# Normalising z2 on ScalarE instead of VectorE, and adding one with a two-tensor operation, in a gated cross-attention and mixture-of-experts kernel

## The chip, the cores and the metric

One Trainium2 chip (trn2), one core. The metric is device time in microseconds, lower is better. A run is one launch of the whole kernel; the time of a kernel is the median of its runs.

## The reference

For each of B = 32 sequences of S = 112 rows and D = 256 columns the kernel computes a gated cross-attention on a context of 375 rows, adds it to x, and then runs a mixture of eight experts (each row takes its best two) on the normalised result:

```
x = x + tanh(g_xattn[0]) * xattn(ctx, layernorm(x), mask)    # 8 heads of 64, keys = context and latents
z2 = layernorm(x)                                            # (x - mean) / sqrt(var + eps)
bids = sigmoid(z2 @ conf_w.T + conf_b) * wealth              # 8 experts
top_bids, chosen = top_k(bids, 2);  weights = softmax(top_bids)
x = x + tanh(g_ffn[0]) * sum over chosen experts of weight * (silu(z2 Wg) * (z2 Wu)) Wd
```

## The kernel before

Everything on the five engines is written out by hand with semaphores; the order of each engine's instructions is the order of the text. There are two stages.

The **attention stage** (to about 1150 us of the span) is a loop over sequences, called batches here, two to an iteration of the loop (parity `p`). A turn of `body(b, p)` has eight steps `h`, one per head. In step h the engines work on several batches at once: TensorE (PE) makes the scores of batch b (`sims`, tile simP), the projections of batch b + 1 (`piece`, tile fP), the transposes of the probabilities (`probs_T`, ptP) and the products with the values (`values`, oP) of heads two and three back, and it finishes batch b - 1: transposing the heads' outputs (`heads_T`), the output projection (`out_proj`), and in step 7 the transpose of z2 (`norm2_T`, line 1271). VectorE (DVE) takes the masked maximum of the scores (`masked_max`, L833), on which the exponentials on ScalarE (ACT, L635) wait, and it makes the low halves of every split number (L823, L839). PE's `sims` of the next batch wait for the masked maximum of head 7 of this one (semaphore s_max).

The **path to z2** of batch b - 1: in step 5 VectorE adds the residual, takes the statistics (L863 to L870: x1, then mean and variance in mv1); GpSimd (POOL) makes 1/sqrt(var + eps) in rs1 (`rstd1`, L464 and L467); in step 6 VectorE normalises x1 to z2 (`norm2`, L876); in step 7 PE transposes z2 (L1271). Behind `rstd1` in POOL's own order stands `split_weights`: two long instructions (L474, L477) that split a 128x1536 piece of the experts' weights into a high and a low part, one piece per batch. ScalarE in step 6 normalises the second half of a later batch's rows (`norm_rows`, L602 and L603).

The **routing** is done for a pair of batches, in odd turns from b = 3 on: VectorE's chain `choose` (steps 2 to 4), `route_rank` (step 5), `route_weights` (step 6, L936 to L943: small tiles of 112x2 and 112x16) and `route_place` (step 7), each link waiting for the one before. `route_weights` stands ahead of the masked maximum of head 7 in VectorE's order.

The **expert stage** then runs 63 tiles of 128 routed rows through the experts, weights streamed by DMA.

The tiles of the change: `rs1` (per row: var + eps, 1/sqrt), `mv1`, `x1`, `z2` (printed as z in the profile), `gexp` and `w1` (printed as w), and `ones`, a tile of ones in SBUF that the kernel already has.

Of the kernel before, what the change touches and what calls it, by code (L numbers as in the profile page):

```python
# [5 lines left out]
F32 = mybir.dt.float32  # L6
# [4 lines left out]
ALU = mybir.AluOpType  # L11
ACT = mybir.ActivationFunctionType
# [3 lines left out]
B, S, D = 32, 112, 256  # L16
# [48 lines left out]
def build(nc, x, ctxt, mask, scal, lnw, wqkv, wout, confw, confbw, wffn, out):  # L65
# [4 lines left out]
    with ctx:  # L70
        def sem(name):
            return ctx.enter_context(nc.semaphore(name))

        def sb(name, shape, dt, stack=ctx):
            return stack.enter_context(nc.sbuf_tensor(name, shape, dt))

        def psum(name, shape, stack):
# [6 lines left out]
        minus_half = sb("minus_half", [P, 4], F32)  # L84
# [33 lines left out]
        x1 = [sb(f"x1_{i}", [S, D], F32) for i in range(2)]  # L118
# [13 lines left out]
        gexp = sb("gexp", [S, 2], F32)  # L132
        w1 = sb("w1", [S, 2], F32)
# [6 lines left out]
        pa = ExitStack()  # L140
# [16 lines left out]
        ones = sb("ones", [P, P], F32, pa)  # L157
# [25 lines left out]
        aoT = sb("aoT", [P, 2, MB, S], F32R, pa)  # L183
        bn1 = sb("bn1", [S, 6], F32, pa)
        mv1 = sb("mv1", [S, 2], F32, pa)
        rs1 = sb("rs1", [S, 2], F32, pa)
        z2 = [sb(f"z2_{i}", [S, D], F32, pa) for i in range(2)]
        z2T = sb("z2T", [P, KD, S], F32, pa)
        wstage = wr[:, :, :].rearrange("p a c -> p (a c)")[:, 0:WCH]
# [54 lines left out]
        s_bn1, s_mv1, s_rch1, s_rs1, s_z2, s_z2t, s_z2c, s_logit, s_lg = [sem(n) for n in (  # L244
            "s_bn1", "s_mv1", "s_rch1", "s_rs1", "s_z2", "s_z2t", "s_z2c", "s_logit", "s_lg")]

        s_rexp, s_route, s_oh, s_gexp, s_rank, s_slots, s_zcopy, s_scat = [sem(n) for n in (
            "s_rexp", "s_route", "s_oh", "s_gexp", "s_rank", "s_slots", "s_zcopy", "s_scat")]
# [11 lines left out]
        def need(eng, semaphore, count):  # L260

            if not isinstance(count, int) or count > 0:
                eng.wait_ge(semaphore, count)

        def apart(eng):

            eng.sem_inc(s_carry, 1)

        def holds(b, lo, hi):

            return lo <= b <= hi if isinstance(b, int) else True
# [7 lines left out]
        def zseq(b, k):  # L279

            return k if isinstance(b, int) and b == 0 else seq(b - 2, PZ + k)
# [112 lines left out]
        def _(pool):  # L394
# [66 lines left out]
            def rstd1(b):  # L461
                pool.wait_ge(s_mv1, b + 1)
                apart(pool)
                nc.gpsimd.tensor_scalar(rs1[:, 0:1], mv1[:, 1:2], EPS, None, ALU.add).then_inc(s_rch1, 1)  # L464
                pool.wait_ge(s_rch1, b + 1)
                apart(pool)
                nc.gpsimd.tensor_tensor(rs1[:, 1:2], rs1[:, 0:1], minus_half[0:S, 0:1], ALU.pow).then_inc(s_rs1, 1)  # L467

            def split_weights(b):

# [105 lines left out]
        def _(act):  # L576
# [17 lines left out]
            def norm_rows(b, p, part):  # L594

                if part == 0:
                    act.wait_ge(s_rstd, b + 1)
                    need(act, s_piece, 0 if isinstance(b, int) and b == 0 else zseq(b - 1, KD - 1) + 1)
                    for i in range(2):
                        nc.scalar.activation(z[0:CP, i, :], xc[p][:, i, :], ACT.Identity, bias=shift[0:CP, i:i + 1], scale=rs[0:CP, i:i + 1])  # L600
                else:
                    nc.scalar.activation(z[0:CP, 2, :], xc[p][:, 2, :], ACT.Identity, bias=shift[0:CP, 2:3], scale=rs[0:CP, 2:3])  # L602
                    nc.scalar.activation(z[0:S, 3, :], xl[p][:, :], ACT.Identity, bias=shift[0:S, 3:4], scale=rs[0:S, 3:4]).then_inc(s_z, 1)  # L603
# [40 lines left out]
            def heads_out_hi(b):  # L644
                act.wait_ge(s_aot, b + 1)
                nc.scalar.activation(aoT[:, 0, :, :], aoT_P, ACT.Copy).then_inc(s_aohi, 1)

            def norm2_out(b):
                act.wait_ge(s_z2t, b + 1)
                nc.scalar.activation(z2T[:, :, :], z2T_P, ACT.Copy).then_inc(s_z2c, 1)  # L650
# [18 lines left out]
            def body(b, p, last_pair=None):  # L669
                for h in range(H):  # L670
                    if h == 4 and holds(b, 1, B):
                        heads_out_hi(b - 1)
                    if holds(b, 0, B - 3):
                        if h == 1:
                            rows_out(b + 2)
                        if h == 2:
                            rows_hi(b + 2, p)
                    if holds(b, 0, B - 2):
                        for n in SLOT_PIECES.get(h, []):
                            piece_hi(b + 1, 1 - p, n)  # L680
                    if h < 2 and holds(b, 1, B):
                        probs_hi(b - 1, H - 2 + h)
                    if h >= 2 and holds(b, 0, B - 1):
                        probs_hi(b, h - 2)
                    if holds(b, 0, B - 1):
                        exps(b, p, h)
                    if h == 7 and holds(b, 1, B):
                        norm2_out(b - 1)
                    if h in (5, 6) and holds(b, 0, B - 4):
                        norm_rows(b + 3, 1 - p, h - 5)  # L690
                    if h == 5 and holds(b, 2, B + 1):
                        copy_rows(b - 2, p, (b - 2) // 2 if isinstance(b, int) else last_pair)
                    if p == 1 and holds(b, 3, B + 1):
                        pair_ = (b - 3) // 2 if isinstance(b, int) else last_pair
                        if h == 1:
                            route_exps(pair_)
                        if h == 5:
                            route_gap(pair_)
# [71 lines left out]
        def _(dve):  # L770
# [98 lines left out]
                apart(dve)  # L869
                nc.vector.bn_aggr(mv1[:, :], bn1[:, :]).then_inc(s_mv1, 1)  # L870

            def norm2(b, p):

                dve.wait_ge(s_rs1, b + 1)
                need(dve, s_zcopy, b - 1)
                nc.vector.tensor_scalar(z2[p][:, :], x1[p][:, :], mv1[:, 0:1], rs1[:, 1:2], ALU.subtract, ALU.mult).then_inc(s_z2, 1)  # L876

            def per_expert(ap):
                return ap.unsqueeze(1).to_broadcast([S, 2, E])

# [9 lines left out]
            def link(ins):  # L890
                chain[0] += 1
                ins.then_inc(s_route, 1)
# [40 lines left out]
            def route_weights(pair):  # L933

                dve.wait_ge(s_gexp, pair + 1)
                link(nc.vector.tensor_scalar(w1[:, :], gexp[:, :], 1.0, None, ALU.add))  # L936
                after_last(pair)
                link(nc.vector.tensor_tensor(slot[:, :, :], tmp[:, :, :], per_expert(regoff_b[:, :]), ALU.add))
                link(nc.vector.reciprocal(w1[:, :], w1[:, :]))
                after_last(pair)  # L940
                link(nc.vector.tensor_scalar(wt[:, 0, :], w1[:, :], gates[0:S, 1:2], None, ALU.mult))
                after_last(pair)
                link(nc.vector.tensor_tensor(wt[:, 1, :], wt[:, 0, :], gexp[:, :], ALU.mult))  # L943
# [50 lines left out]
            def body(b, p, j=None):  # L994
                for h in range(H):
# [23 lines left out]
                            piece_lo(b + 1, 1 - p, n)  # L1019
                    if h == 4 and holds(b, 1, B):  # L1020
                        heads_out_lo(b - 1)
                    if h == 6 and holds(b, 1, B):
                        norm2(b - 1, 1 - p)
                    choose_some(1)
                    if h == 5 and routing:

# [436 lines left out]
```

## Time and profile before

| | us |
|---|---|
| median of 3 runs | 1826.02 (1825.33 to 1826.6) |
| the profiled execution: time | 1822.79 |
| its span, first to last instruction | 1821.2 |
| TensorE busy | 1618.4 (89%) |
| VectorE busy | 1015.1 (56%) |
| ScalarE busy | 844.4 (46%) |
| GpSimd busy | 611.8 (34%) |
| mean granted clock of TensorE, as a share of its full speed | 0.92 |

The span is what the rows of the trace cover; the 1.6 us between it and the time of the same execution lie around it. An engine's busy time says how much it worked, not who waited for it: for that the waits and the order of time are read. Reading the clock: 1.00 means 2.4 GHz, 0.50 means 1.2 GHz, a number between them is a stretch with some of both.

### The profile page before, as it was taken

To read this page: it belongs to the slowest core of one execution; us is meant where nothing else is said; L and a number is where in the kernel's file an instruction comes from. 1 tells how busy PE (TensorE), PEld (TensorE's weight loads), DVE (VectorE), ACT (ScalarE), POOL (GpSimd) and SP (SyncE) were. 2 spreads that over 40 slices of the span, in tenths; PEclk is the share of its full clock that TensorE was granted. 3 is DMA by queue.
4 is the path that set the end of the run, shared out by engine and by line. 5 is a ranking of instruction groups with operands and counts; after the bars stand their busy time and mean duration, and the time that the engine had idled before them with its cause. 6 is when DMAs were issued, how large, how long until landed. Compare 5 with 4: busy or idle time off the path is not lost.

```text
span 1821.2 us, 39638 instructions
## 1 busy us (share of the span) xinstructions
PE 1618.4 (89%) x11946; PEld 1378.0 (76%) x11947; DVE 1015.1 (56%) x2655; ACT 844.4 (46%) x1856; POOL 611.8 (34%) x663
## 2 busy tenths in 40 slices
PE   1898988988988988988988987699999989999965
PEld 1687877877877877877877876578888878888855
DVE  4478678678678678678678666322333223333321
ACT  2576656656656656656656644222333222332221
POOL 4344434434434434434434432112222222222211
PEclk9899889889889889889889887799999999999987
DMA  2142322422322322322322324681111375111173
GB/s 88 44 137 73 137 88 75 134 86 78 131 86 79 130 86 79 131 85 80 130 85 81 114 103 138 215 254 26 29 26 29 89 236 167 26 26 29 28 213 95
DMA packets 70908, 180.59 MB, mean 99 GB/s; under 512 B 11664, under 2 KB 33552, under 8 KB 70864
## 3 DMA queue, kind: packets, MB, share of 16 engines
q1 hardware_dynamic: 54464, 153.66, 25.3%
q0 software_dynamic: 15264, 24.25, 6.6%
q10 hardware_dynamic: 1136, 2.12, 0.4%
q8 instruction: 24, 0.39, 0.1%
q14 instruction: 20, 0.16, 0.0%
HBM read 106.91 MB, written 73.09 MB: 99 GB/s over the span
## 4 chain that ended last, share of the span: by engine, by line
PE 68%; DVE 11%; DMA 7%; issue 7%; ACT 4%; POOL 1%; SPq 1%; DVEq 0%; POOLq 0%; ACTq 0%
PE fP L1184 19%; PE yP L1184 9%; PE gP L1184 8%; PE uP L1184 8%; PE simP L1232 5%; PE ptP L1242 4%; DMA W<-split_experts 3%; PE oP L1184 3%; PE aP L1370 2%; PE tP L1184 2%; DVE w L936 2%; DVE z L876 2%; DMA out<-ysb,xt 2%; PE fP L1200 2%; DMA xt<-routed_rows 1%
## 5 line engine op out<-in xcount | busy, mean ns | idle before, releaser
L1184 PE MATMUL fP<-zTs,ws 128*128 128x112 f32 (+1 forms) x1536 | 324.5, 369 | 1.0 <-DVE zT L810 0.9
L1184 PEld LDWEIGHTS fP<-zTs,ws 128*128 128x128 f32 x1536 | 261.7, 222 | 51.8 <-issue 31.1
L1123 DVE TENSOR_TENSOR act_h<-uP,sg 128x512 f32<-128x512 f32 x126 | 87.1, 691 | 289.2 <-ACT sg L731 289.2
L1184 PE MATMUL gP<-W,xT 128*128 (+1 forms) x756 | 210.9, 415 | 33.5 <-issue 27.0
L1184 PE MATMUL fP<-ws,zTs 128*122 128x512 f32 x768 | 207.2, 405 | 4.7 <-DVE kT L823 4.7
L731 ACT ACTIVATE sg<-gP 128x512 f32<-128x512 f32 x126 | 75.3, 597 | 289.9 <-PE uP L1184 289.9
L635 ACT ACTIVATE pr<-ms,nmax 112x488 f32<-112x488 f32 x256 | 179.3, 700 | 65.4 <-DVE nmax L833 65.2
L1184 PEld LDWEIGHTS yP<-W,aT 128*128 128x128 f32 x1512 | 192.5, 194 | 10.1 <-issue 5.3
L1184 PE MATMUL yP<-W,aT 128*128 (+1 forms) x1512 | 194.3, 286 | 4.6 <-DVE aT L1127 4.6
L1184 PE MATMUL uP<-W,xT 128*128 (+1 forms) x756 | 196.1, 395 | 0.0
L547 POOL DMA_INDIRECT out<-ysb,xt x63 | 100.6, 1596 | 270.5 <-ACT ysb L743 254.7
L833 DVE CUSTOM_DVE_ANT_0 ms<-simP,madd 112x488 f32<-112x488 f32 x256 | 169.4, 662 | 30.3 <-PE simP L1232 14.7
L1232 PE MATMUL simP<-kT,qT 64*112 64x488 f32 x768 | 135.5, 463 | 55.0 <-DVE nmax L833 54.4
L1184 PEld LDWEIGHTS gP<-W,xT 128*128 128x128 f32 x756 | 135.7, 192 | 59.8 <-issue 37.6
L1127 DVE TENSOR_TENSOR aT<-aP,aT 128x512 fp32r<-128x512 f32 x126 | 86.4, 686 | 164.7 <-ACT aT L737 164.7
L839 DVE SCALAR_TENSOR_TENSOR pT<-ptP,pT 122x448 f16<-122x448 f32 x256 | 157.9, 617 | 31.1 <-ACT pT L642 22.6
L642 ACT ACTIVATE pT<-ptP 122x448 f16<-122x448 f32 x256 | 138.2, 540 | 73.7 <-PE ptP L1242 65.2
L1184 PEld LDWEIGHTS uP<-W,xT 128*128 128x128 f32 x756 | 145.1, 192 | 32.2
L1184 PEld LDWEIGHTS fP<-ws,zTs 128*122 128x122 f32 x768 | 133.1, 183 | 45.8 <-issue 12.4
L1184 PE MATMUL oP<-v,pT 122*128 122x64 f16 x3072 | 142.8, 199 | 15.5 <-DVE ao L851 13.8
L737 ACT ACTIVATE aT<-aP 128x512 fp32r<-128x512 f32 x126 | 75.0, 595 | 172.4 <-PE aP L1370 172.4
L1242 PE MATMUL ptP<-ident,pr 112*122 112x112 f32 x1024 | 154.6, 277 | 0.0
(196 smaller groups left out, 2508.3 us busy)
## 6 DMA issues: line engine op xcount, KB each, us to landing
split_experts<-wparts SPq DMA_DIRECT2D x32, 1536.0 KB
W<-split_experts SPq DMA_DIRECT2D x64, 768.0 KB
wr<-wffn SPq DMA_DIRECT2D x32, 768.0 KB
xc<-ctxt SPq DMA_DIRECT2D x32, 375.0 KB
xt<-routed_rows POOLq DMA_DIRECT2D x63, 129.0 KB, 2.4
xl<-x SPq DMA_DIRECT2D x32, 112.0 KB
xres<-x SPq DMA_DIRECT2D x32, 112.0 KB, 7.9
out<-x SPq DMA_DIRECT2D x32, 112.0 KB, 1.9
```

The lines of the kernel that those rows point to most:

```text
L547: pool.indirect_dma_start(out[:, :], bass.IndirectOffsetOnAxis(ap=xt[k][:, D:D + 1].bitcast(I32), axis=0), ysb[k % 2][:, :], None, compute ...
L635: nc.scalar.activation(pr[h % 2][:, :], ms[h % 2][:, :], ACT.Exp, bias=nmax[p][:, h:h + 1], scale=-1.0, accum_out=rsum[p][:, h:h + 1]).the ...
L642: nc.scalar.activation(pT[h % 2][:, 0, :, 0:S], ptP[h % 2][0:KR, :, 0:S], ACT.Copy, scale=P_TOP).then_inc(s_pthi, 1)
L731: nc.scalar.activation(sg[i][:, :], gP[i][:, :], ACT.Silu).then_inc(s_silu, 1)
L737: nc.scalar.activation(aT[q][i][:, 0, :, :], aP[i][:, :, :], ACT.Copy).then_inc(s_athi, 1)
L833: nc.vector.tensor_tensor_reduce(out=ms[h % 2][:, :], in0=simP[h % 2][0:S, 0:NK], in1=madd[p][:, :], scale=-SCALE, scalar=3.0e38, op0=ALU. ...
L839: nc.vector.scalar_tensor_tensor(out=pT[h % 2][:, 1, :, 0:S], in0=ptP[h % 2][0:KR, :, 0:S], scalar=P_TOP, in1=pT[h % 2][:, 0, :, 0:S], op0 ...
L1123: nc.vector.tensor_tensor(act_h[i][:, :], uP[i][:, :], sg[i][:, :], ALU.mult).then_inc(s_act, 1)
L1127: nc.vector.tensor_tensor(aT[q][i][:, 1, :, :], aP[i][:, :, :], aT[q][i][:, 0, :, :].bitcast(F32), ALU.subtract).then_inc(s_atlo, 1)
L1184: last = nc.tensor.matmul(o, lhs(k, a), rhs(k, c), start=n == 0, stop=n == len(todo) - 1)
L1232: last = nc.tensor.matmul(simP[i][0:S, 0:NK], qT[p][r, a, h // 2, :], kT[p][r, c, h // 2, :], start=t == 0, stop=t == len(PARTS) - 1)
L1242: last = nc.tensor.transpose(ptP[h % 2][0:KR, c, 0:S], pr[h % 2][:, c * KR:(c + 1) * KR], ident[0:S, 0:S])
```

## The change

Four things are changed.

- `norm2` moves from VectorE to ScalarE. It was (x1 - mean) * rstd as one `tensor_scalar`; it becomes an activation with a scale and a bias per row, x1 * rstd + (-mean * rstd).
- GpSimd's `rstd1` gets two more small instructions that make the bias (mean * rstd, then times -1) in a third column of rs1, each waiting for the one before.
- On ScalarE `norm2` stands at the end of step 6, behind the exponentials and `norm_rows`; on VectorE it stood in step 6 behind `piece_lo` and ahead of `probs_lo`.
- In `route_weights` the addition of 1.0 to gexp, a `tensor_scalar`, becomes a `tensor_tensor` of gexp and a 112x2 part of `ones`.

```
-        rs1 = sb("rs1", [S, 2], F32, pa)
+        rs1 = sb("rs1", [S, 3], F32, pa)
...
                 nc.gpsimd.tensor_scalar(rs1[:, 0:1], mv1[:, 1:2], EPS, None, ALU.add).then_inc(s_rch1, 1)
-                pool.wait_ge(s_rch1, b + 1)
+                pool.wait_ge(s_rch1, b * 3 + 1)
                 apart(pool)
-                nc.gpsimd.tensor_tensor(rs1[:, 1:2], rs1[:, 0:1], minus_half[0:S, 0:1], ALU.pow).then_inc(s_rs1, 1)
+                nc.gpsimd.tensor_tensor(rs1[:, 1:2], rs1[:, 0:1], minus_half[0:S, 0:1], ALU.pow).then_inc(s_rch1, 1)
+                pool.wait_ge(s_rch1, b * 3 + 2)
+                nc.gpsimd.tensor_tensor(rs1[:, 2:3], mv1[:, 0:1], rs1[:, 1:2], ALU.mult).then_inc(s_rch1, 1)
+                pool.wait_ge(s_rch1, b * 3 + 3)
+                apart(pool)
+                nc.gpsimd.tensor_scalar(rs1[:, 2:3], rs1[:, 2:3], -1.0, None, ALU.mult).then_inc(s_rs1, 1)
...
+            def norm2(b, p):
+
+                act.wait_ge(s_rs1, b + 1)
+                nc.scalar.activation(z2[p][:, :], x1[p][:, :], ACT.Identity, bias=rs1[:, 2:3], scale=rs1[:, 1:2]).then_inc(s_z2, 1)
...
                     if h in (5, 6) and holds(b, 0, B - 4):
                         norm_rows(b + 3, 1 - p, h - 5)
+                    if h == 6 and holds(b, 1, B):
+                        norm2(b - 1, 1 - p)
...
-            def norm2(b, p):
-
-                dve.wait_ge(s_rs1, b + 1)
-                need(dve, s_zcopy, b - 1)
-                nc.vector.tensor_scalar(z2[p][:, :], x1[p][:, :], mv1[:, 0:1], rs1[:, 1:2], ALU.subtract, ALU.mult).then_inc(s_z2, 1)
-
...
-                link(nc.vector.tensor_scalar(w1[:, :], gexp[:, :], 1.0, None, ALU.add))
+                link(nc.vector.tensor_tensor(w1[:, :], gexp[:, :], ones[0:S, 0:2], ALU.add))
...
                     if h == 4 and holds(b, 1, B):
                         heads_out_lo(b - 1)
-                    if h == 6 and holds(b, 1, B):
-                        norm2(b - 1, 1 - p)
                     choose_some(1)
```

VectorE in the loop, steps 6 and 7 of an odd turn, before the change:

```order
L823 TENSOR_TENSOR v<-fP,v 122x512 [waits s_phi]
L876 TENSOR_SCALAR z_0<-x_0,mv,rs 112x256 [waits s_zcopy,s_rs1]
L839 SCALAR_TENSOR_TENSOR pT<-ptP,pT 122x4x112 [waits s_pthi]
L936 TENSOR_SCALAR w<-gexp 112x2 [waits s_gexp]
L263 REGISTER_ALU
L938 TENSOR_TENSOR slot<-tmp,regoff_b 112x16 [waits s_route]
L939 RECIPROCAL w<-w 112x2
```

L876 is the instruction that leaves this engine, and L936 the one that is rewritten. The same place with the change, up to the masked maximum of head 7:

```order
L835 TENSOR_TENSOR v<-fP,v 122x512 [waits s_phi]
L851 SCALAR_TENSOR_TENSOR pT<-ptP,pT 122x4x112 [waits s_pthi]
L942 TENSOR_TENSOR w<-gexp,ones 112x2 [waits s_gexp]
L263 REGISTER_ALU
L944 TENSOR_TENSOR slot<-tmp,regoff_b 112x16 [waits s_route]
L945 RECIPROCAL w<-w 112x2
L263 REGISTER_ALU
L947 TENSOR_SCALAR wt<-w,gates 112x2 [waits s_route]
L263 REGISTER_ALU
L949 TENSOR_TENSOR wt<-wt,gexp 112x2 [waits s_route]
L840 REGISTER_ALU
L845 ISA ms,nmax<-simP,madd 112x488 [waits s_sim,s_exp]
```

The normalisation of z2 (z_0<-x_0) is gone, and the first link of `route_weights` has two inputs; the four links behind it are as they were.

ScalarE in the loop, steps 6 and 7 of an odd turn, with the change (exponentials of head 6, then the second half of `norm_rows`, then step 7):

```order
L640 ACTIVATE pr,rsum<-ms,nmax 112x488 [waits s_pt,s_max]
L607 ACTIVATE z<-xc,shift,rs 125x256
L608 ACTIVATE z<-xl,shift,rs 112x256
L656 ACTIVATE z_0<-x_0,rs 112x256 [waits s_rs1]
L625 REGISTER_ALU
L633 ACTIVATE v<-fP 122x512 [waits s_piece]
L647 ACTIVATE pT<-ptP 122x4x112 [waits s_pv,s_pt]
```

L656 is the added instruction; the others stand as before.

GpSimd in the loop, `rstd1` and `split_weights` of an odd turn, with the change:

```order
L464 TENSOR_SCALAR rs<-mv 112x1 [waits s_mv1]
L465 ISA
L467 TENSOR_TENSOR rs<-rs,minus_half 112x1 [waits s_rch1]
L468 REGISTER_ALU
L469 TENSOR_TENSOR rs<-mv,rs 112x1 [waits s_rch1]
L470 REGISTER_ALU
L472 TENSOR_SCALAR rs<-rs 112x1 [waits s_rch1]
L476 ISA
L479 CAST wparts<-wr 128x1536 [waits s_wst,s_wput]
L482 TENSOR_TENSOR wparts<-wr,wparts 128x1536 [waits s_whi]
```

L469 and L472 are new, and stand ahead of the two long instructions of `split_weights` (L474 and L477 before).

## Rows read from the trace of the kernel before

**Rows 1.** The page, part 1: busy time, share, instructions of each engine.
```profile
PE 1618.4 (89%) x11946; PEld 1378.0 (76%) x11947; DVE 1015.1 (56%) x2655; ACT 844.4 (46%) x1856; POOL 611.8 (34%) x663
```

**Rows 2.** The waits: who waited for whom; us in total, times, longest.
```profile
PE simP L1232 <- DVE nmax L833: 54.4, 14, 4.0
PE tP L1271 <- DVE z L876: 19.3, 31, 5.0
```

**Rows 3.** Timeline, an odd turn: start us, duration us, instruction [idle before <-releaser].
```profile
516.27 1.47 POOL L474 CAST wparts<-wr 128x1536 fp32r<-128x1536 f32 x1
516.48 1.40 DVE L876 TENSOR_SCALAR z<-x,mv,rs 112x256 f32<-112x256 f32 x1
...
517.34 0.59 ACT L603 ACTIVATE z<-xl,shift,rs 112x256 f32<-112x256 f32 x1
...
517.91 3.43 POOL L477 TENSOR_TENSOR wparts<-wr,wparts 128x1536 fp32r<-128x1536 f32 x1 [0.18 <-POOL wparts L474]
...
517.94 0.41 PE L1271 MATMUL tP<-ident,z 112*128 112x112 f32 x2 [0.54 <-DVE z L876]
...
518.34 3.03 DVE L936 TENSOR_SCALAR w<-gexp 112x2 f32<-112x2 f32 x1
...
521.69 0.23 DVE L941 TENSOR_SCALAR wt<-w,gates 112x2 f32<-112x2 f32 x1
...
522.23 0.67 DVE L833 CUSTOM_DVE_ANT_0 ms<-simP,madd 112x488 f32<-112x488 f32 x1
...
522.96 1.56 PE L1232 MATMUL simP<-kT,qT 64*112 64x488 f32 x6 [3.88 <-DVE nmax L833]
```

**Rows 4.** Windows: length, busy of each engine, then granted clock, DMA share, GB/s.
```profile
179.00:183.00 4.00, 0.09 (x5) 0.01 (x2) 3.74 (x8) 0.34 (x2) 2.34 (x1) 0.80 0.12 47
519.00:523.00 4.00, 0.12 (x5) 0.04 (x2) 3.77 (x8) 0.37 (x2) 2.34 (x1) 0.96 0.06 25
523.00:536.00 13.00, 13.00 (x80) 11.83 (x80) 6.64 (x25) 5.72 (x14) 5.11 (x5) 0.50 0.73 260
```

**Rows 5.** Timeline, VectorE beside a long instruction of GpSimd, in step 3.
```profile
497.85 2.80 POOL L450 TENSOR_TENSOR zTs<-zT,zTs 128x1200 fp32r<-128x1200 f32 x1 [5.46 <-ACT zTs L616]
...
500.21 0.47 DVE L906 TENSOR_TENSOR bids<-bids,confb 112x16 f32<-112x16 f32 x1
...
506.92 0.17 DVE L914 TENSOR_TENSOR tmp<-bids,top 112x16 f32<-112x16 f32 x1
```

**Rows 6.** Timeline, GpSimd's small instructions of another chain, like the two added.
```profile
509.87 0.19 POOL L442 TENSOR_TENSOR rs<-rs,rs_t 128x1 f32<-128x1 f32 x1 [0.18 <-POOL rs_t L441]
...
510.63 0.24 POOL L444 TENSOR_SCALAR shift<-shift 128x4 f32<-128x4 f32 x1 [0.20 <-POOL shift L443]
```

**Rows 7.** Timeline, an even turn, step 6.
```profile
555.59 0.59 ACT L603 ACTIVATE z<-xl,shift,rs 112x256 f32<-112x256 f32 x1
...
555.92 0.41 PE L1271 MATMUL tP<-ident,z 112*128 112x112 f32 x2 [0.26 <-DVE z L876]
```

**Rows 8.** Timeline, GpSimd L464, a mark that returns in every turn.
```profile
117.20 0.23 POOL L464 TENSOR_SCALAR rs<-mv 112x1 f32<-112x1 f32 x1 [3.56 <-DVE mv L870]
...
145.03 0.23 POOL L464 TENSOR_SCALAR rs<-mv 112x1 f32<-112x1 f32 x1 [3.39 <-DVE mv L870]
...
175.33 0.23 POOL L464 TENSOR_SCALAR rs<-mv 112x1 f32<-112x1 f32 x1 [4.25 <-DVE mv L870]
...
212.67 0.23 POOL L464 TENSOR_SCALAR rs<-mv 112x1 f32<-112x1 f32 x1 [3.40 <-DVE mv L870]
...
826.34 0.23 POOL L464 TENSOR_SCALAR rs<-mv 112x1 f32<-112x1 f32 x1 [3.40 <-DVE mv L870]
```

**Rows 9.** Timeline, the end of the attention stage.
```profile
1125.89 0.63 PE L1271 MATMUL tP<-ident,z 112*128 112x112 f32 x2 [5.05 <-DVE z L876]
...
1157.71 2.90 PE L1184 MATMUL gP<-W,xT 128*128 128x512 f32 x6 [6.22 <-DMA W<-split_experts]
```

## The prediction

> **What bounds the kernel now.** I read the busy times first: TensorE works 1618.4 us of a span of 1821.2, VectorE 56% [rows 1]. So time can only come from TensorE's gaps or its clock. The waits name the gaps that touch this change [rows 2]: 14 times TensorE waits some 3.9 us before the scores (simP) for VectorE's masked maximum, 54.4 us in all, and 31 times it waits for z2, 19.3 us in all. The timeline of an odd turn shows why the first is so long [rows 3]. VectorE's addition of one on 112x2 numbers starts at 518.34 and lasts 3.03 us; it ends at 521.37, and GpSimd's subtraction L477 ends at 521.34. The normalisation of z2 just before it lasts 1.40 us and ends at 517.88, 0.14 us behind the end of GpSimd's cast L474. Both VectorE instructions are held by GpSimd's, not by their own work. Behind L936 come four small links, and only then, at 522.23, the masked maximum that TensorE waits for; TensorE goes on at 522.96. The gap has a second price: the clock falls to 1.2 GHz in it and stays there for some 13 us [rows 4].
>
> What that costs in all follows from the returns of L464 [rows 8]. From batch 1 to 2, with no routing and no stall, a turn takes 145.03 - 117.20 = 27.83 us; the next, with half of a routing chain, 30.30; and the one with stall and slow clock 212.67 - 175.33 = 37.34. Later a pair of turns takes (826.34 - 212.67) / 9 = 68.19 us against 27.83 + 30.30 = 58.13. The stall and its slow clock are worth 10.06 us per pair, 141 us in 14 pairs. The whole question is whether the change removes them.
>
> **The addition as a two-tensor operation.** This is meant for L936, so the question is whether GpSimd holds such an operation too. The nearest row is L906 [rows 5]: a tensor_tensor of 112x16, both inputs in SBUF, started 2.36 us into GpSimd's L450. It lasts 0.47 us and ends at 500.68, 0.03 us behind L450's end at 500.65; the same form, L914, takes 0.17 us when no long instruction of GpSimd runs. So it is held, and gexp with ones is of the same kind. The Trainium skill, in "SBUF — State Buffer", section "Who interferes with whom", has this as a rule that speaks against the change: a VectorE instruction with two SBUF inputs contends with a GpSimd instruction that reads SBUF, and the later one blocks fully. The trace agrees.
>
> Even if the new form were free, the links behind it are not: L938 and L943 have two SBUF inputs, and L941 is a tensor_scalar of 112x2 like L936. They show no hold now only because L477 is over when they start. So I place the new chain against GpSimd. GpSimd's two added instructions are like 0.19 with 0.18 us ahead, and 0.24 with 0.20 ahead [rows 6]: 0.81 us. L474 then runs 517.08 to 518.55 and L477 518.73 to 522.16. VectorE, rid of z2, comes to the addition 518.34 - 1.32 = 517.02, since L839 and what follows now start where the normalisation started (L839 at 516.48 instead of 517.80). From the addition to the masked maximum it takes some 1.0 us unheld (L941 starts 0.32 behind L936's end, L833 0.54 behind that). That fits neither ahead of L474 nor into the 0.18 us between L474 and L477. So some link is caught by L477 until 522.16. If it is L941, which the gap makes likeliest, the masked maximum starts 0.33 us later: 522.49 instead of 522.23, **+0.26 us**. The bounds are 0.0 (only L943 caught) and +0.8 (L938 caught, the old tail of 0.86 us behind 522.16).
>
> **z2 on ScalarE.** ScalarE's L603 is the same operation on the same shape: 0.59 us, the next instruction following it 0.5 us after its start. rs1 is there in time, at 517.12 against ScalarE free at 517.84. In an even turn L603 starts at 555.59 [rows 7]; z2 is then done at 555.59 + 0.49 + 0.59 = 556.67 and TensorE transposes at 556.72, not 555.92: **+0.80 us**. Nothing covers it: TensorE stands in order behind this transpose and has no other wait up to the next batch's scores. Fifteen turns have it (b = 1 and the even ones from 2 to 28): 12.0 us. In the 14 odd turns the same delay is 517.34 + 1.13 = 518.47 against 517.94, +0.53 us, and is hidden: three small products later TensorE waits for the masked maximum anyway. If the stall went, this cover would go too. The 1.1 us that VectorE gains in even turns is worth nothing, since the masked maximum of head 7 is not what TensorE waits for there. ScalarE gets 32 x 0.6 us = 19 us on 844.
>
> GpSimd's 0.81 us also moves what is queued behind it, the split, the store of its parts and SP's later loads; they have over 10 us until they are needed. In the last two turns the path through GpSimd is bare (TensorE idle 5.05 us before the transpose at 1125.89), so z2 comes about 1 us later each time, but the experts' first product then waits 6.22 us for its weights [rows 9], which do not depend on z2: 0. Batch 30 adds 0.2.
>
> **Sum without the clock:** 12.0 + 14 x 0.26 + 0.2 = 15.8 us.
>
> **What the clock gives back.** In the first stall the clock is at half for 1.6 us of the four (0.80), in a late one for 0.3 us (0.96) [rows 4]. The slow stretch is about as long each time, so what of it falls into the idle time costs nothing. The pair with the first stall takes 212.67 - 145.03 = 67.64 us, a late one 68.2 [rows 8]: 1.3 us more of idle slow time saves about 0.6 us, 0.45 per us. And the pairs settle at one length and stay there for the rest of the stage. I read this as a balance: when a pair is longer, the fall comes earlier in the next gap and the pair gets shorter. With 1.06 us more per pair the balance needs the fall 1.06 / 0.45 = 2.4 us earlier, 2.7 us before TensorE goes on, still inside a gap of about 3.6 us. It can be reached. Then only the way there is paid (2.4 us), the 1.6 us of batches 1 and 2, ahead of the first stall, and 0.5 for the end: **+4.5 us**. To keep 15.8 the balance would have to fail. Bounds: 1 and 16, with a tail to 20 from the +0.8 bound of the odd turns. I take +4.5, nearer the lower end, because the rows show settling.
>
> Against the profiled execution this makes 1822.8 + 4.5 = 1827.3. The median of the runs lies 3.2 us above it, so 1830.5, rounded up for the longer tail: **1831 us**. What can be told from no change is 0.2%, 3.7 us.
>
> **Rivals.**
> 1. *The clock gives nothing back*: the stall stays and each pair pays its 1.06 us. 1826 + 9 to 22, about 1842. For it: the balance rests on a few pair lengths. Chance 22%.
> 2. *The stall goes* (the other side): GpSimd's split doesn't hold the small chain, the masked maximum starts near 518. Then 141 us are saved and 15 x 0.80 + 14 x 0.53 = 19.4 paid back, since the cover of the odd turns is gone: 1826 - 122 = 1704. It decides at the single point whether L947 and L949 (112x2) are held by L482. For it: L936 and L876, the two held instructions of this place, are the two that are rewritten. Against it: L906, and L941's kinship with L936. 8%.
> 3. *The clock falls in the even turns too*, because TensorE's gap there grows from 0.26 to 1.07 us: another 5.6 us (37.34 - 27.83 - 3.9) in 15 turns, 1915. Against it: the 0.54 us gap of the odd turns [rows 3] brings no fall by itself; the clock is still full at the start of the stall [rows 4]. 4%.
> 4. *It does nothing that can be measured*: z2's 0.80 us finds cover that I don't see. 1826. 4%.
>
> **The numbers.** The forecast has 62%: split at 3.7 us into 28 "same" and 33 "slower", 1 below. With the rivals: faster 0.09, same 0.32, slower 0.59. The range 1824 to 1844 takes the forecast and most of rival 1, and leaves out rivals 2 and 3 and the far tail.
>
> **What would show it.** Right: the new addition L942 or a link behind it lasts 1 to 3 us and ends with L479 or L482; TensorE still waits some 14 times before simP for the masked maximum, 3.5 to 4 us each; TensorE's wait before L1271's successor goes from 0.26 to about 1.1 us in even turns; late pairs of turns keep near 68.2 us and the clock stands at half for over 2 us of the stall. Wrong: late pairs at 69 us or more (rival 1), all five links at 0.15 to 0.25 us and no wait before simP (rival 2), stretches at 1.2 GHz in even turns (rival 3).

## The result and the profile after

| | before | after |
|---|---|---|
| median, us | 1826.31 (1825.33 to 1827.6, 4 runs) | 1837.96 (1836.6 to 1840.22, 4 runs) |
| the profiled execution: time, span | 1822.79, 1821.2 | 1840.22, 1838.6 |
| mean granted clock | 0.92 | 0.919 |

The change costs 11.65 us: the ratio is 1.0069, with a 95% interval of 1.0054 to 1.0083. That is inside the range of 1824 to 1844, on the side of "slower", and 7 us above the forecast of 1831. The two profiled executions lie on opposite sides of their medians, so their spans differ by more, 17.4 us; what is read from the two traces is to be taken with that in mind.

Busy times of after, the page's part 1 (for [rows 1]):

```profile
PE 1616.6 (88%) x11946; PEld 1376.8 (75%) x11947; DVE 1004.1 (55%) x2623; ACT 859.8 (47%) x1888; POOL 625.3 (34%) x727
```

Only 11 us have left VectorE, though the normalisation had been 37.7 us of it (32 times L876): its two held links, the addition and the product with the gates, have grown from 46.4 to 67.3 us. 15 us have come to ScalarE and 13.5 to GpSimd (its two new instructions, 64 in all); TensorE's own work is the same. So the loss is in its gaps or its clock. Waits of after (for [rows 2]; us in total, times, longest):

```profile
PE simP L1236 <- DVE nmax L845: 49.9, 14, 4.2
PE tP L1275 <- ACT z L656: 40.3, 31, 5.9
```

The stall before the scores is still there 14 times, a little shorter each time (3.5 us instead of 3.9). The wait for z2 has doubled. The timeline of an odd turn of after (for [rows 3]; start, duration, instruction, in brackets idle before and its releaser) shows who holds whom now:

```profile
526.40 0.24 POOL L472 TENSOR_SCALAR rs<-rs 112x1 f32<-112x1 f32 x1 [0.20 <-POOL rs L469]
526.61 1.46 POOL L479 CAST wparts<-wr 128x1536 fp32r<-128x1536 f32 x1
526.64 1.45 DVE L942 TENSOR_TENSOR w<-gexp,ones 112x2 f32<-112x2 f32 x1
526.97 0.59 ACT L608 ACTIVATE z<-xl,shift,rs 112x256 f32<-112x256 f32 x1
527.46 0.59 ACT L656 ACTIVATE z<-x,rs 112x256 f32<-112x256 f32 x1
...
528.11 0.41 PE L1275 MATMUL tP<-ident,z 112*128 112x112 f32 x2 [1.07 <-ACT z L656]
...
528.12 0.17 DVE L944 TENSOR_TENSOR slot<-tmp,regoff_b 112x16 f32<-112x16 f32 x1
528.22 0.15 DVE L945 RECIPROCAL w<-w 112x2 f32<-112x2 f32 x1
528.26 3.43 POOL L482 TENSOR_TENSOR wparts<-wr,wparts 128x1536 fp32r<-128x1536 f32 x1 [0.19 <-POOL wparts L479]
528.41 3.30 DVE L947 TENSOR_SCALAR wt<-w,gates 112x2 f32<-112x2 f32 x1
...
532.03 0.67 DVE L845 CUSTOM_DVE_ANT_0 ms<-simP,madd 112x488 f32<-112x488 f32 x1
...
532.76 0.75 PE L1236 MATMUL simP<-kT,qT 64*112 64x488 f32 x2 [3.51 <-DVE nmax L845]
```

The addition, now of two tensors, starts 0.03 us behind GpSimd's cast L479 and ends 0.02 us behind it: 1.45 us for 224 numbers. Of the links behind it, L944 starts in the gap between L479 and L482, and L945, a reciprocal with one input, starts 0.04 us ahead of L482 and takes 0.15 us. The next, L947, starts behind L482 and ends 0.02 us behind it. So both forms are held, `tensor_tensor` and `tensor_scalar`, and the hold was passed on to the next link. The Trainium skill's rule, "SBUF — State Buffer", section "Who interferes with whom", names two inputs in SBUF for a block; L942 agrees with it.

An even turn of after, its timeline (for [rows 7]), shows TensorE's wait for z2 at 1.06 us, where it was 0.26:

```profile
565.36 0.59 ACT L656 ACTIVATE z<-x,rs 112x256 f32<-112x256 f32 x1
...
566.01 0.41 PE L1275 MATMUL tP<-ident,z 112*128 112x112 f32 x2 [1.06 <-ACT z L656]
```

And the mark L464, in the timeline of GpSimd in after (for [rows 8]):

```profile
424.58 0.23 POOL L464 TENSOR_SCALAR rs<-mv 112x1 f32<-112x1 f32 x1 [3.42 <-DVE mv L882]
455.72 0.23 POOL L464 TENSOR_SCALAR rs<-mv 112x1 f32<-112x1 f32 x1 [4.54 <-DVE mv L882]
493.79 0.23 POOL L464 TENSOR_SCALAR rs<-mv 112x1 f32<-112x1 f32 x1 [3.39 <-DVE mv L882]
562.61 0.23 POOL L464 TENSOR_SCALAR rs<-mv 112x1 f32<-112x1 f32 x1 [3.42 <-DVE mv L882]
631.22 0.23 POOL L464 TENSOR_SCALAR rs<-mv 112x1 f32<-112x1 f32 x1 [3.43 <-DVE mv L882]
701.18 0.23 POOL L464 TENSOR_SCALAR rs<-mv 112x1 f32<-112x1 f32 x1 [3.42 <-DVE mv L882]
977.62 0.23 POOL L464 TENSOR_SCALAR rs<-mv 112x1 f32<-112x1 f32 x1 [3.38 <-DVE mv L882]
```

An even turn takes 455.72 - 424.58 = 31.14 us, where before had 30.30. Pairs of turns take 69.21, 68.82, 68.61 and then 69.96 us, and so on in the same cycle: (977.62 - 424.58) / 8 = 69.13 on average, against 68.2 in [rows 8]. The pairs no longer keep one length. (In the trace of before they take 68.2 to 68.4 us from 417 on.) What the clock does in them is seen in windows of after around two stalls, the one at 532 and the one two pairs later (columns as in [rows 4]):

```profile
528.00:530.00 2.00, 1.15 (x18) 1.03 (x18) 1.93 (x4) 1.08 (x3) 1.81 (x2) 1.00 0.00 0
530.00:532.00 2.00, 0.00 (x0) 0.00 (x0) 1.87 (x2) 0.00 (x0) 1.69 (x1) 0.87 0.00 0
...
544.00:546.00 2.00, 2.00 (x21) 1.52 (x19) 1.39 (x4) 1.84 (x5) 0.00 (x0) 0.72 0.34 103
...
667.00:669.00 2.00, 0.00 (x0) 0.00 (x0) 2.00 (x1) 0.00 (x0) 2.00 (x1) 0.75 0.00 0
669.00:671.00 2.00, 0.78 (x4) 0.68 (x6) 1.84 (x6) 0.80 (x3) 0.15 (x1) 0.50 0.23 95
...
684.00:686.00 2.00, 2.00 (x8) 1.65 (x9) 0.79 (x3) 0.14 (x2) 1.73 (x1) 0.73 0.00 0
```

A clock of 0.87 over 530 to 532 is 0.5 us at half: it fell near 531.5, and rose again near 545.1, after 13.6 us. At the later stall it fell at 668.0 and rose at 685.1, after 17.1 us. The table gives the same reading, from windows of 1 us, for successive odd turns of three kernels (the third is an experiment below). "Lead" is how long before TensorE went on the clock fell.

| | lead of the fall, us | half clock, us | from one rise to the next, us |
|---|---|---|---|
| before, seven pairs from 454.74 | 0.30, 0.26, 0.28, 0.28, 0.32, 0.28, 0.22 | 13.7 each | 68.3 each |
| after, from 463.52 | 0.32, 1.30, 1.82, 2.22, 0.44, 1.40, 1.88, 2.22 | 13.7, 13.7, 13.7, 17.1, 13.7, 13.7, 13.7, 17.1 | 68.3 to the next of 13.7; 71.7 to one of 17.1 |
| before with 12 more transposes in step 7 (`e10`), from 459.51 | -1.76, -2.08, -2.44, 0.60, -1.88, -2.26, 0.78 | 10.2, 10.3, 10.2, 13.7, 10.2, 10.2, 13.7 | 68.3 each |

So in these rows the rises stand 68.3 us apart, and a pair of turns that is a little longer than that comes a little later each time against the fall. In after this goes on up to a lead of 2.2 us. Then the slow stretch comes out 3.4 us longer and ends 71.7 us after the last, and the lead starts anew. The step lies at the same place in the other rows with a stall of 3.5 us: in after and in `e2` (below) every lead up to 1.98 us has a stretch of 13.7, and every one from 2.02 us on has 17.1, as has the first of `e9`, at 2.23. These are readings of records; why a stretch comes in these lengths no run here tells. Nor is 68.3 us a rhythm that the clock keeps by itself: at the end of the stage in before a rise follows the last one after 34.1 us.

### The profile page after: what moved, and what is told of

It reads as the page before. It is cut to its first block, busy times and chain, and to the rows that moved or that the text cites. A ratio compares the mean times of both kernels' runs of the same rounds, so it can differ in the third digit from the quotient of the medians.

```text
span 1838.6 us, 39781 instructions
## 1 busy us (share of the span) xinstructions
PE 1616.6 (88%) x11946; PEld 1376.8 (75%) x11947; DVE 1004.1 (55%) x2623; ACT 859.8 (47%) x1888; POOL 625.3 (34%) x727
## 4 chain that ended last, share of the span: by engine, by line
PE 66%; DVE 11%; DMA 8%; issue 7%; ACT 5%; POOL 1%; SPq 1%; DVEq 0%; POOLq 0%; ACTq 0%
PE fP L1188 19%; PE yP L1188 9%; PE gP L1188 8%; PE uP L1188 8%; PE simP L1236 5%; DMA W<-split_experts 5%; PE ptP L1246 4%; PE oP L1188 3%; DVE wt L947 3%; PE aP L1374 2%; PE tP L1188 2%; PE fP L1204 2%; DMA out<-ysb,xt 1%; DVE w L942 1%; DMA xt<-routed_rows 1%
## 5 line engine op out<-in xcount | busy, mean ns | idle before, releaser
L1188 PE MATMUL fP<-zTs,ws 128*128 128x112 f32 (+1 forms) x1536 | 329.6, 373 | 0.9 <-DVE zT L822 0.9
L1188 PEld LDWEIGHTS fP<-zTs,ws 128*128 128x128 f32 x1536 | 266.4, 226 | 51.4 <-issue 30.1
L1236 PE MATMUL simP<-kT,qT 64*112 64x488 f32 x768 | 132.8, 455 | 50.5 <-DVE nmax L845 49.9
L1188 PE MATMUL oP<-v,pT 122*128 122x64 f16 x3072 | 142.1, 199 | 16.6 <-DVE ao L863 14.9
```

Source lines behind the costliest of these rows:

```text
L1188: last = nc.tensor.matmul(o, lhs(k, a), rhs(k, c), start=n == 0, stop=n == len(todo) - 1)
L1236: last = nc.tensor.matmul(simP[i][0:S, 0:NK], qT[p][r, a, h // 2, :], kT[p][r, c, h // 2, :], start=t == 0, stop=t == len(PARTS) - 1)
```

## The experiments

**1. Is it the addition's form, or z2's move?** One part of the change at a time, and a third kernel that mends the new wait. `e1` is before with the new addition alone:

```
-                link(nc.vector.tensor_scalar(w1[:, :], gexp[:, :], 1.0, None, ALU.add))
+                link(nc.vector.tensor_tensor(w1[:, :], gexp[:, :], ones[0:S, 0:2], ALU.add))
```

> The kernel before with nothing but the addition written as a two-tensor operation. Theory (GpSimd's split holds both forms): the addition still starts some 0.5 us behind the normalisation, still lasts 3.0 us and ends with GpSimd's subtraction; time as before, 1826 us, within 3. Rival (the two-tensor form is not held, only tensor_scalar is): the addition takes 0.16 us and the hold of about 2.7 us moves to the tensor_scalar with the gates, the time again near 1826; the durations of the two instructions tell them apart. If neither is held the time is 1690 to 1710.

Measured: 1826.52 us against 1824.99, ratio 1.0011 (0.9996 to 1.0026). Groups by line of `e1`:

```profile
L936 DVE TENSOR_TENSOR w<-gexp,ones 112x2 f32<-112x2 f32 x16 | 42.6, 2664 | 0.0
```

In before the same group has 42.7 us. The form of the addition changes nothing that can be measured, and the stall is as in [rows 2]: 54.3 us in 14 waits.

`e2` is the changed kernel with that line undone, so only z2's move is left:

> The changed kernel with the addition as a tensor_scalar again, so only the normalisation has moved. Theory (the slowdown is all from the move): 1838 us, within 3, with the addition held 1.4 us by GpSimd's cast and the tensor_scalar with the gates 3.3 us by its subtraction. Rival (the two-tensor form costs time): 1830 us or less.

Measured: 1836.37 us, ratio 1.0058 (1.004 to 1.0075), all of the loss. Groups by line of `e2`:

```profile
L947 DVE TENSOR_SCALAR wt<-w,gates 112x2 f32<-112x2 f32 x16 | 46.5, 2909 | 0.6
L942 DVE TENSOR_SCALAR w<-gexp 112x2 f32<-112x2 f32 x16 | 20.7, 1294 | 0.0
```

The hold is passed on from the addition to L947 here too: what moved it is the time at which the chain starts, not how its first link is written.

`e3` is the changed kernel with z2 ahead of the rows' normalisation in ScalarE's step 6:

```
+                    if h == 6 and holds(b, 1, B):
+                        norm2(b - 1, 1 - p)
                     if h in (5, 6) and holds(b, 0, B - 4):
                         norm_rows(b + 3, 1 - p, h - 5)
-                    if h == 6 and holds(b, 1, B):
-                        norm2(b - 1, 1 - p)
```

> The changed kernel with the normalisation of z2 ahead of norm_rows in step 6 on ScalarE, not behind it. Theory (15 even turns pay 0.8 us each because z2 stands behind two instructions of ScalarE): TensorE's gap before the transpose of z2 falls from 1.07 us to 0.3 or less, and the time to 1826 to 1831 us. Rival (the slowdown is GpSimd's longer chain and the clock): 1836 us or more.

Measured: 1825.02 us, ratio 0.9997 (0.998 to 1.0013). The loss is gone. Waits of `e3`:

```profile
PE simP L1236 <- DVE nmax L845: 60.0, 14, 4.4
PE tP L1275 <- ACT z L656: 15.9, 16, 5.9
```

The wait for z2 is left only in the odd turns and at the ends, and even turns take 30.2 us. So what the change costs is the place of z2 in ScalarE's order. Note the first line: the stall is 5.6 us longer in all than before's (4.28 us instead of 3.88 in a turn), and pairs still keep 68.2 to 68.4 us. This is no proof of the prediction's balance, since TensorE also waits less for z2: 0.3 us in a pair instead of 0.54 + 0.26. In all it waits as long as in before, 4.6 us of a pair against 4.7.

**2. What are stall and slow clock worth, and what cures them?** In `e4` the changed kernel lets GpSimd scatter first and split the weights behind it, in the odd turns with routing:

```
-                if holds(b, 0, B - 3):
+                late = p == 1 and holds(b, 3, B + 1)
+                if holds(b, 0, B - 3) and not late:
                     split_weights(b)
-                if p == 1 and holds(b, 3, B + 1):
+                if late:
                     scatter(...)
+                if holds(b, 0, B - 3) and late:
+                    split_weights(b)
```

> The changed kernel with GpSimd's split of the weights behind the scatter in the odd turns with routing, so that neither the cast nor the subtraction runs beside the chain of route_weights. Theory (GpSimd's long instructions are what holds the chain, the chain makes TensorE's stall, and the stall makes the clock fall): all five links take 0.15 to 0.25 us, TensorE no longer waits 3.5 us before simP, the clock stays at 2.4 GHz through the middle of the attention stage, time 1690 to 1725 us. Rival (the small instructions are slow for another reason, or another wait takes the stall's place): over 1790 us.

Measured: 1712.45 us, ratio 0.9381 (0.9359 to 0.9402). Groups by line of `e4`, and a window over 860 us of its attention stage:

```profile
L950 DVE TENSOR_SCALAR wt<-w,gates 112x2 f32<-112x2 f32 x16 | 3.7, 228 | 0.6
...
L945 DVE TENSOR_TENSOR w<-gexp,ones 112x2 f32<-112x2 f32 x16 | 2.4, 151 | 0.0
```

```profile
100.00:960.00 860.00, 811.73 (x7486) 676.72 (x7486) 655.20 (x1988) 597.63 (x1354) 422.60 (x507) 1.00 0.32 110
```

With no long instruction of GpSimd beside it, the chain runs at 0.15 to 0.23 us a link on average, the stall is gone from the waits, and the clock stays at 1.00. Odd turns take 28.35 us where after has 37.5 to 38.9. The prediction's rival 2 had priced just this at 1704.

`e5` is the same edit on before, `e6` on `e3`, with z2 placed first:

> The kernel before (z2 on VectorE, addition as tensor_scalar) with GpSimd's split behind the scatter in the odd turns with routing. Theory (the hold comes from the split's place, not from the form of the additions): no link of the chain is held, no stall; and without the moved normalisation's 0.8 us in even and 1.1 us in odd turns it beats the same edit on the changed kernel (1712 us) by 20 to 30 us: 1680 to 1695 us. Rival (the changed forms were needed for the gain): some link or z2 still held 1 us or more, over 1712 us.

> The changed kernel with both cures: the normalisation of z2 first in step 6 on ScalarE, the split behind the scatter. Theory: z2 is ready within 0.1 us of TensorE's need in both parities, TensorE's waits before its transpose fall under 0.3 us a turn, 1678 to 1692 us, level with or a little under z2 on VectorE, which in even turns is still held by the cast. Rival (ScalarE's later exponentials or norm_rows become the wait): over 1700 us.

Measured: `e5` 1697.23 us, ratio 0.9296 (0.9262 to 0.9331), slightly above what was expected; one turn of its trace, near 416, still shows a fall of the clock and takes 32.56 us instead of 27.87. `e6` 1687.63 us, ratio 0.9244 (0.9219 to 0.9269), as expected. Turns take 30.29 and 27.87 us in `e5`, 30.18 and 27.56 in `e6`, 31.2 and 28.35 in `e4`. Waits of `e6` and of `e5`, in this order:

```profile
PE tP L1278 <- ACT z L659: 19.1, 17, 5.9
```

```profile
PE tP L1274 <- DVE z L879: 15.1, 18, 5.0
PE simP L1235 <- DVE nmax L836: 10.6, 14, 0.9
```

`e6` is the best version, 139 us faster than before. Once the hold is gone, moving z2 to ScalarE is a gain of 9.6 us over `e5`: TensorE's waits before the scores, up to 0.9 us each, go away. Pairs of turns are 0.4 us shorter, some 6 us in 14; the one fall of the clock in `e5` is another 4.7 in its trace. And z2's place is worth 24.8 us between `e4` and `e6`, twice as much as beside the stall, since the odd turns have lost their cover.

**3. The same cure from VectorE's side.** `e8` leaves GpSimd alone and puts the chain of weights behind head 7's masked maximum:

```
-                        if h == 6:
-                            route_weights(pair_)
                         if h == 7:
+                            route_weights(pair_)
                             route_place(pair_)
```

> The changed kernel with route_weights in step 7, behind the masked maximum of head 7, instead of ahead of it; GpSimd's split stays. Theory (what costs is who stands behind the held link on VectorE): one link is still held 1.4 to 3.3 us, but TensorE's wait before simP shrinks to under 2 us and the clock doesn't fall: 1730 to 1770 us. Rival (the same stall one step later): TensorE waits over 3 us for the masked maximum of head 0 or for VectorE's low halves and the clock falls, over 1810 us.

Measured: 1728.21 us, ratio 0.9457 (0.9437 to 0.9477), 2 us under what was expected. Groups by line, then waits, of `e8`:

```profile
L942 DVE TENSOR_TENSOR w<-gexp,ones 112x2 f32<-112x2 f32 x16 | 24.6, 1534 | 0.0
...
L947 DVE TENSOR_SCALAR wt<-w,gates 112x2 f32<-112x2 f32 x16 | 3.6, 228 | 0.6
```

```profile
PE fP L1203 <- DVE qT L835: 28.6, 15, 6.9
```

The addition is still held, 1.5 us on average, and yet the time is 98 us under before and 110 under after: TensorE's stall before the scores is gone from the waits. Two things have changed at once, though. Nobody on TensorE waits for the held link, and the hold itself is shorter: 28.2 us for L942 and L947 together where after has 67.3, as the chain now meets only the end of L482. That is 2.8 us less in a turn with routing, and a hold that much shorter could by itself take most of the 3.5 us stall away; no run separates the two. It isn't free: TensorE's waits for qT are 28.6 us, of which 15.8 in 13 waits lie in the loop, where after has none. And in the loop the clock still falls for 3.4 us once in three pairs of turns; the expectation had it not fall.

**4. Is the clock's fall the price, or the stall?** In `e7` the changed kernel has TensorE run 18 small products behind z2's transpose in the odd turns with routing; nobody reads them, and nothing is left out:

```
+                    if h == 7 and p == 1 and holds(b, 3, B - 3):
+                        for _ in range(18):
+                            nc.tensor.matmul(ptP[0][0:S, 0, S:P], ident[0:S, 0:S], ident[0:S, 0:P - S], start=True, stop=True)
```

> The changed kernel with 18 small matmuls on constants behind step 7 of the odd turns with routing, whose result nobody reads; they fill most of TensorE's stall. Theory (the stall has two prices, the idle time and the fall to 1.2 GHz that it brings): VectorE's hold and the wait for the masked maximum stay as they are, the clock stays at 2.4 GHz, and the time falls by some 5 to 6 us in each of 13 turns: 1757 to 1775 us. Rival (such small matmuls don't keep the clock up, or the slow stretch costs little): 1830 us or more.

Measured: 1852.61 us, ratio 1.0142 (1.0119 to 1.0164). The expectation was missed. Timeline, then a window, of `e7`:

```profile
461.11 5.58 PE L1325 MATMUL ptP<-ident 112*112 112x16 f32 x36
466.62 1.56 PE L1236 MATMUL simP<-kT,qT 64*112 64x488 f32 x6
```

```profile
461.00:468.00 7.00, 7.00 (x52) 6.33 (x48) 5.55 (x16) 1.55 (x4) 3.08 (x2) 0.61 0.42 169
```

The products took 5.58 us and outlasted the stall they were to fill, and the granted clock was 0.61 in a stretch in which TensorE is recorded as busy all the time. So it tells nothing of the stall alone. `e11` does it again with 14 wide products on the weights' staging tile, unread as well (`range(14)`, 128x112 by 512 columns; the tile is of type fp32r, where `e7` multiplied fp32):

> The changed kernel with 14 matmuls of 512 columns on constant weights in the same place, some 3.0 us at the full clock, results read by nobody, so that they end before the masked maximum comes. Theory (the run with 18 small matmuls failed because they were too narrow to keep the clock up and because they outlasted the stall): the clock stays at 2.4 GHz through the middle of the attention stage, VectorE's hold of 3.3 us stays, odd turns fall from 38.0 to 32 to 33 us, time 1755 to 1780 us. Rival (filling can't keep the clock, whatever the matmuls): falls of the clock in every odd turn and 1830 us or more.

Measured: 1808.59 us against 1824.37, ratio 0.9913 (0.9888 to 0.9938). Timeline, then a window, of `e11`:

```profile
449.68 3.35 DVE L947 TENSOR_SCALAR wt<-w,gates 112x2 f32<-112x2 f32 x1
...
450.36 3.50 PE L1325 MATMUL ptP<-ws 128*112 128x512 f32 x14
454.08 0.95 PE L1236 MATMUL simP<-kT,qT 64*112 64x488 f32 x6 [0.22 <-DVE nmax L845]
```

```profile
100.00:1040.00 940.00, 858.14 (x7523) 705.12 (x7522) 700.73 (x1946) 590.91 (x1333) 418.70 (x501) 0.99 0.30 100
```

Here the clock stays up for the most part with the hold in place: eight stretches of 3.4 us at half are left in the 940 us. Only 29 us come back; 1755 to 1780 had been expected. Odd turns take 34.8 to 36.5 us, still far from 28.35. TensorE now waits elsewhere (waits of `e11`):

```profile
PE fP L1188 <- DVE zT L822: 30.0, 14, 2.5
```

After has this wait once, with 0.9 us. I take it that the slow clock had hidden it: the two holds have cost VectorE 1.45 + 3.30 - 0.15 - 0.23 = 4.4 us, and as long as TensorE runs at half, VectorE can catch up unseen. That is argued, not shown. So of the 9 us of a pair (126 us between after and `e4`, in 14) about 2 (29 us) come back with the clock alone, and most go with the hold. An estimate of the 96 us that are left, from these rows: the stall itself, 49.9 us in after, is still there and only filled with useless work; the wait for zT is 30.0 us; and the eight stretches at half cost up to 8 x 3.4 / 2 = 14 us.

**5. Does the balance hold, and how far?** In `e9` and `e10`, before runs z2's two transposes three or seven times over (the same values into the same place), which makes every turn longer on TensorE:

```
-                for k in range(KD):
+                for k in list(range(KD)) * 3:
```

> The kernel before with the two transposes of z2 done three times over, about 0.4 us more of TensorE in every turn, hidden in the odd turns with the stall. Theory of the balance (a longer pair brings the clock's fall earlier in the stall, and the pair keeps its length): pairs of turns settle at 68.3 us again with the fall about 0.9 us earlier, the time rises by 3 us or less. Rival (no balance): the late pairs take 68.6 to 68.7 us and the time rises by 6 us or more.

> The kernel before with the two transposes of z2 done seven times over, about 1.2 us more of TensorE in every turn. Theory (the balance has an end: when the fall would have to come so early that TensorE had not yet been idle long enough, it is missed and comes later, with a longer slow stretch): pairs of 68.3 us are broken every few pairs by one some 3 us longer, as in the changed kernel, mean near 69.2, the time rises by 10 to 17 us. Rival 1 (the balance holds): 68.3 us throughout, under 5 us. Rival 2 (no balance): all pairs alike at 69.4 or more, 17 us or more.

Timeline of an even turn of `e9`, then of `e10`:

```profile
559.65 0.79 PE L1271 MATMUL tP<-ident,z 112*128 112x112 f32 x6 [0.26 <-DVE z L876]
```

```profile
558.91 1.56 PE L1271 MATMUL tP<-ident,z 112*128 112x112 f32 x14 [0.24 <-DVE z L876]
```

Against 0.41 us in [rows 7] an even turn is up to 0.38 us longer in `e9`, and up to 1.15 in `e10`; by the mark L464 even turns take 30.64 and 31.42 us, where before has 30.3. Measured: `e9` 1830.7 us against 1824.98, ratio 1.0022 (1.0005 to 1.0038), a rise of 5.7 us where 3 or less had been expected and 6 or more by the rival; `e10` 1823.99 us, ratio 1.0006 (0.9991 to 1.0021), where 10 to 17 us had been expected. The late pairs of `e9` take 68.27 us, with the fall 0.90 us ahead of TensorE's going on instead of 0.28: a new balance at the old length, reached step by step from -0.26, 0.12, 0.46, 0.67 and 0.81 us. So the theory is right in the length of the pairs, and the rival is wrong in it. Of the loss, the way there makes 3.8 us in the trace (the third last mark L464 at 1102.31 us against 1098.51 in before), the first slow stretch, of 17.1 us, above all; where the rest lies the trace, the slowest of ten runs, doesn't show. The mark L464 of `e10`, timeline of GpSimd:

```profile
420.44 0.23 POOL L464 TENSOR_SCALAR rs<-mv 112x1 f32<-112x1 f32 x1 [3.42 <-DVE mv L870]
...
488.39 0.23 POOL L464 TENSOR_SCALAR rs<-mv 112x1 f32<-112x1 f32 x1 [3.40 <-DVE mv L870]
...
556.30 0.23 POOL L464 TENSOR_SCALAR rs<-mv 112x1 f32<-112x1 f32 x1 [3.42 <-DVE mv L870]
...
624.18 0.23 POOL L464 TENSOR_SCALAR rs<-mv 112x1 f32<-112x1 f32 x1 [3.39 <-DVE mv L870]
...
693.39 0.23 POOL L464 TENSOR_SCALAR rs<-mv 112x1 f32<-112x1 f32 x1 [3.40 <-DVE mv L870]
```

Its pairs take 67.95, 67.91, 67.88 and 69.21 us, 68.24 on average: the length of before. As the table above shows, the slow stretch here is 10.2 us in three pairs of four or two of three, so 3.4 us shorter than before's, and one of 13.7 us puts it back in step. In after it is the other way round, 13.7 with one of 17.1. Some 1.1 us more per pair is given back in the one and not in the other, and the records differ in where the fall stands against the stall: behind it in most pairs of `e10`, in it in after. They also differ in what was added, work of TensorE in the one and idle time in the other; no run separates the two. The expectation for `e10` had the longer stretches of after, and was missed.

## Why the prediction was right, and where it was off

- *The addition as a two-tensor operation stays held*: right, `e1` and L942. Shown.
- *Which link is caught*: right. L479 ran 526.61 to 528.07 and L947 was the link that L482 caught, with one difference: the addition started 0.03 us behind L479's start and was itself held until 528.09. I had it start 0.06 us ahead.
- *+0.26 us in the odd turns*: the right sign, too large. The time from TensorE's readiness for z2's transpose to its going on with the scores is 522.96 - (517.94 - 0.54) = 5.56 us in [rows 3] and 532.76 - (528.11 - 1.07) = 5.72 in after, so +0.16. TensorE's stall went from 3.9 to 3.5 us because the late z2 lets TensorE reach it 0.53 us later.
- *z2 on ScalarE, +0.80 us in each of 15 even turns*: right. Even turns are 31.14 to 31.20 us instead of 30.30, +0.86; the wait went from 0.26 to 1.06 (I expected 1.1). `e3` shows the rest of the step: it is the place in ScalarE's order, not the engine.
- *End of the stage at nothing*: it fits. The last two waits for z2 grew to 5.94 and 4.08 us, and behind them the experts' first product waits 7.33 us for its weights, where [rows 9] have 6.22. From the third last mark L464 to this product it is 59.2 us in before and 59.3 in after, and 60.1 in `e1`, which leaves z2 alone: the end varies by more than was asked of it.
- *Stall and slow clock are worth 10.06 us per pair*: right in all. Pairs take 58.16 us in `e5` where before has 68.2, and the medians give 129 us for 14 pairs, against 141 (rival 2's 1704 stood against 1712 for `e4`). I had taken no split between the two; by `e11` most goes with the hold.
- **The step that failed is "What the clock gives back", the +4.5.** The sum of 15.8 us without the clock nearly holds: with the measured 0.86 and 0.16 it would be 15 x 0.86 + 14 x 0.16 + 0.2 = 15.3. The balance is real in its place: in before the leads go 1.61, 0.96, 0.58, 0.39, 0.30 and stay, and `e9` (late pairs) and `e10` (on average) keep 68.2 to 68.3 us per pair through 0.4 and 1.1 us of added work. What failed is "It can be reached". I asked for a fall 2.7 us before TensorE goes on and looked only at whether this lies inside the gap. Pairs of after do go that way: 69.21, 68.82 and 68.61 us at leads of 0.32, 1.30 and 1.82, so 0.4 us shorter per us of lead, where I had 0.45. But I took the slow stretch to be "about as long each time", and from a lead of 2.0 on it is 17.1 us instead of 13.7. That pair takes 69.96, the lead starts again at 0.4, and the 2.7 that the balance needs is never reached. So a pair is 0.87 us longer on average, not 0, and the clock gives back only 0.15 of the 0.86 + 0.16 = 1.02 us: this is rival 1, which had said 1842 and "late pairs at 69 us or more". By the medians 15.3 - 11.65 = 3.7 us come back in all, against the 11 that I had counted on; by the two traces, whose loops differ by 14.9 us from the first mark L464 to the third last, still less.
- *The range* of 1824 to 1844 held, and that is in part luck. It took in rival 1, to which I had given 22% and whose mechanism came, while the 1831 rests on the term that failed.
- *Rivals 3 and 4* didn't occur: the clock falls once a pair, as before.

Open: why slow stretches come in lengths of 10.2, 13.7 and 17.1 us, and what makes the one of 17.1 from a lead of 2.0 us on; that it is the idle time of TensorE behind the fall is only argued. No kernel with more or less idle time at the same lead was run.

## What to carry to other kernels

A small VectorE instruction that lasts as long as GpSimd's long one beside it is not cured by writing it in another form, nor by starting it earlier: the next link is caught. Place the long instruction where nobody on VectorE is waited for (`e4` to `e6`, 7.6% with z2 placed well), or let the instruction that others wait for go ahead of the chain (`e8`, 5.4%, with a shorter hold as well). When an operation moves to another engine, its place in that engine's order decides: the same z2 cost 12 us at the end of ScalarE's step, nothing at its start, and there it gained 9.6 us once the stall was gone.

## What was not expected of the hardware

- The clock's rises were 68.3 us apart in before, `e9` and `e10`, whether the slow stretch was 10.2 or 13.7 us, and 71.7 us apart where after had one of 17.1. The pairs of turns of these three kernels, 68.2 us long and each with a stall, stayed in step with them, and added work of 0.4 and 1.1 us per pair left their length as it was (the whole kernels: +5.7 us and -1.0 us). A small change measured in such a loop may look free, or dear, for this reason alone.
- With TensorE recorded as busy for 7.00 of 7.00 us, some 5.5 of them on 16-column products, the granted clock was 0.61 (`e7`). With 512-column products in the same place it was 0.99 over 940 us of the stage, where `e7` has 0.89 (`e11`). Width, number and operand type of the products all differ between the two, so which of them counts isn't shown.
- Filling a stall to keep the clock up gave back 29 us of some 126: the stall's own time stayed, and TensorE then met a wait of 30.0 us in all of which the kernel with the slow clock has 0.9.
